# A two-layer graph kernel with residual and normalisation: its first row block done in four stripes, and column 0 loaded by chunk for four row blocks

## The reference

```
def _layernorm(x, axis=-1, eps=1e-05):
    m = jnp.mean(x, axis=axis, keepdims=True)
    v = jnp.var(x, axis=axis, keepdims=True)
    return (x - m) / jnp.sqrt(v + eps)

x_drop = x * (u >= 0.1) / 0.9                # x, u: (8192, 64)
h = _layernorm(x + adj @ x_drop)             # adj: (8192, 8192), float32
y = _layernorm(h + adj @ (h @ weight) + bias)   # weight: (64, 64)
```

## Time and profile before

| what | value |
|---|---|
| median of 3 runs | 946.46 us (946.38 to 946.99) |
| the profiled execution | 946.82 us |
| its span in the trace | 944.9 us |
| mean granted PE clock | 0.991 of full speed |
| PE busy | 911.6 us |
| DMA | 359.36 MB, 380 GB/s over the span |

### The profile page before, as it was taken

One profiled execution on the slowest core, in us unless ns is written; L12 is line 12 of the kernel. 1 busy time (PEld: TensorE's weight loads), 2 busy tenths in 40 slices (PEclk: granted clock), 3 DMA queues, 4 the chain that ended last, 5 costly groups with the idle time before them and its releaser, 6 DMA issues.

```text
span 944.9 us, 9819 instructions
## 1 busy us (share of the span) xinstructions
PE 911.6 (96%) x4288; PEld 307.0 (32%) x4288; DVE 202.8 (21%) x419; ACT 29.9 (3%) x68; POOL 24.1 (3%) x23
## 2 busy tenths in 40 slices
PE   4689999999999999999999999999999999999996
PEld 1123333333333333333333333333333333333342
DVE  2111121120131221312213120402122121130256
ACT  0010000000000000000000000000000000000011
POOL 2000000000000000000000000000000000000123
PEclk9799999999999999999999999999999999999998
DMA  9999999999969899799999999998989989999951
GB/s 349 402 421 421 419 421 421 421 385 423 420 273 422 335 377 421 307 421 387 349 412 389 421 363 421 368 421 327 422 343 397 420 347 421 420 418 421 395 225 67
DMA packets 57338, 359.36 MB, mean 380 GB/s; under 512 B 6352, under 2 KB 14544, under 8 KB 14544
## 3 DMA queue, kind: packets, MB, share of 16 engines
q1 hardware_dynamic: 57296, 358.74, 93.3%
HBM read 356.61 MB, written 2.10 MB: 380 GB/s over the span
## 4 chain that ended last, share of the span: by engine, by line
PE 92%; DMA 5%; SPq 3%; DVE 1%; issue 0%; ACT 0%; DVEq 0%
PE psum L586 26%; PE psum L631 22%; PE psum L591 21%; PE psum L615 18%; DMA tiles<-adj_t 5%; PE psum L637 3%; SPq L335 2%; PE psum L652 1%; PE psum L667 1%; SPq L314 1%; PE psum L596 0%; SPq L313 0%; DVE vsum L438 0%; DVE layer L544 0%; DVE rstd L444 0%
## 5 line engine op out<-in xcount | busy, mean ns | idle before, releaser
L591 PE MATMUL psum<-tiles,stat 128*64 128x512 f32 x548 | 252.7, 610 | 24.7 <-DMA tiles<-adj_t 24.7
L586 PE MATMUL psum<-tiles,stat 128*64 128x512 f32 x1136 | 253.3, 593 | 0.0
L596 PE MATMUL psum<-tiles,stat 128*64 128x512 f32 x548 | 252.7, 610 | 0.0
L631 PE MATMUL psum<-tiles,stat 128*64 128x512 f32 x944 | 210.7, 593 | 0.0
L474 DVE TENSOR_TENSOR layer<-psum,layer 128x512 f32<-128x512 f32 (+1 forms) x126 | 87.0, 690 | 461.1 <-PE psum L631 213.5
L615 PE MATMUL psum<-tiles,stat 128*64 128x512 f32 x768 | 169.1, 593 | 0.0
L591 PEld LDWEIGHTS psum<-tiles,stat 128*64 128x64 f32 x548 | 75.4, 140 | 191.0 <-issue 150.1
L586 PEld LDWEIGHTS psum<-tiles,stat 128*64 128x64 f32 x1136 | 80.7, 137 | 158.1 <-issue 158.1
L631 PEld LDWEIGHTS psum<-tiles,stat 128*64 128x64 f32 x944 | 67.2, 137 | 131.7 <-issue 130.9
L615 PEld LDWEIGHTS psum<-tiles,stat 128*64 128x64 f32 x768 | 54.8, 137 | 108.0 <-issue 108.0
L596 PEld LDWEIGHTS psum<-tiles,stat 128*64 128x64 f32 x548 | 75.4, 140 | 0.0
(11 more groups left out here) (38 smaller groups left out, 143.3 us busy)
## 6 DMA issues: line engine op xcount, KB each, us to landing
tiles<-adj_t SPq DMA_DIRECT2D x334, 1024.0 KB, 11.4
x_res<-x SPq DMA_DIRECT2D x16, 128.0 KB, 10.6
out<-layer SPq DMA_DIRECT2D x8, 256.0 KB, 2.1
tiles<-u SPq DMA_DIRECT2D x3, 512.0 KB, 14.0
tiles<-x SPq DMA_DIRECT2D x3, 512.0 KB, 15.2
tiles<-u SPq DMA_DIRECT2D x1, 384.0 KB, 6.2
tiles<-x SPq DMA_DIRECT2D x1, 384.0 KB, 7.3
tiles<-u SPq DMA_DIRECT2D x1, 128.0 KB, 2.0
```

What stands on the lines that cost most here:

```text
L586: last = pe.matmul(sum_a[i % 2][to, :], stat[:, j * C + c, half], tile[:, c], start=begun.get(("a", to.start)) != i, stop=False, skip_grou ...
L591: last = pe.matmul(sum_a[i % 2][low, :], stat[:, j * C + c, 0:D], tile[:, c], start=begun.get(("a", 0)) != i, stop=ends and c == 2, skip_g ...
L596: last = pe.matmul(sum_b[i % 2][high, :], stat[:, j * C + c, 0:D], tile[:, c], start=begun.get(("b", D)) != i, stop=ends and c == 3, skip_ ...
L631: last = pe.matmul(bank[to, :], stat[:, j * C + c, D:2 * D], tile[:, c], start=c == 0, stop=c == C - 1)
```

## The change

Row 0 is done in four stripes of 128 output rows. A stripe is four `part` jobs of four columns each, with matmuls that move 128 columns instead of 512 (64 of them in a stripe), and each stripe is copied out (`part_end`), transposed and normalised by itself (`part_turn`). That gives h of column 0 for chunk `c` = stripe alone. The tiles of row 0 come from a second array in HBM, `adj_0`: for columns 4 to 15 one load of 1 MiB holds one stripe of four tiles, and for columns 0 to 3, whose tiles are held whole for layer 2, each tile is loaded in four pieces of 256 KiB. Tiles of column 0 in rows 4 to 15 are no longer loaded whole: a load of 1 MiB takes chunk `c` of four of them, and its two jobs, `chunk` and `rest`, do both layers for two rows each (two halves each). Eight of the twelve such loads are placed into stripes 1 to 3; the `early` pairs of column 0 are gone. x and u are loaded all before the last load of stripe 0.

```diff
-XU_GROUPS = ((4, 5), (5, 8), (8, 12), (12, 16), (0, 4))
-XU_BEFORE = (1, 3, 6, 10)
+PARTS = 4
+XU_GROUPS = ((0, 1), (1, 4), (4, 8), (8, 12), (12, 16))
+XU_BEFORE = (1, 4, 5, 6)
...
+def chunk_jobs(c):
+    return [(kind, g, c) for g in range((NB - EARLY) // PARTS) for kind in ("chunk", "rest")]
...
+    for q in range(PARTS):
+        for g in range(groups):
+            jobs.append(("part", q, g))
+            if q and g == 0:
+                jobs.append(("part_turn", q - 1))
+            elif chunks_due and (q > 1 or g > 1):
+                jobs += chunks_due[:2]
+                chunks_due = chunks_due[2:]
+            if g == 0 and q:
+                chunks_due += chunk_jobs(q - 1)
+        jobs.append(("part_end", q))
+
+    for i in range(1, NB):
...
+        if i == 1:
+            heavy = chunks_due
...
+                if part is not None:
+                    to = tiles[:, slot, :, part * P:(part + 1) * P]
+                    source = adj_0[part, 0, :, tile[1]]
+                elif kind == "part":
+                    to, source = tiles[:, slot], adj_0[tile[1], tile[2]].rearrange("p k c b -> p k (c b)")
+                elif kind == "chunk":
+                    to = tiles[:, slot]
+                    rows = rows_of_chunk(tile[1])
+                    source = adj_t[rows.start:rows.stop, 0, :, tile[2]].rearrange("r p b -> p r b")
+                else:
+                    to, source = tiles[:, slot], adj_t[tile]
...
+                        for c in range(C):
+                            to, sums = (slice(0, D), sum_a) if c % 2 == 0 else (slice(D, P), sum_b)
+                            last = pe.matmul(sums[bank][to, 0:P], stat[:, j * C + c, 0:D], moving[:, c],
+                                             start=j == 0 and c < 2, stop=j == NB - 1 and c >= 2,
+                                             skip_group_check=True)
...
+                    for half in slice(0, D), slice(D, 2 * D):
+                        if n_second >= ECHO_BANKS:
+                            pe.wait_ge(added, n_second - ECHO_BANKS + 1)
+                        bank = echo[n_second % ECHO_BANKS]
+                        n_second += 1
+                        pe.matmul(bank[0:D, :], stat[:, c, half], moving[:, n], start=True, stop=True)
+                        last = pe.matmul(bank[D:P, :], stat[:, c, half], moving[:, n + 1], start=True, stop=True)
+                    last.then_inc(tile_jobs_done, 1)
...
+        "adj_0": np.ascontiguousarray(a[0].reshape(NB // PARTS, PARTS, P, C, PARTS, P).transpose(4, 0, 2, 1, 3, 5)),
```

More of the change, by code:

```diff
@@ L68, in seconds_of, with rows_of_chunk, first_row, turns @@
     return jobs
-TILE_JOBS = ("fused", "first", "second", "pair", "early")
-HALVES = {"first": 1, "second": 1, "fused": 2, "pair": 2, "early": 4}
+TILE_JOBS = ("part", "chunk", "rest", "fused", "first", "second", "pair", "early")
+HALVES = {"part": 1, "chunk": 1, "rest": 1, "first": 1, "second": 1, "fused": 2, "pair": 2, "early": 4}
 def tiles_of(job):
     kind, i, j = job
+    if kind == "part" and j == 0:
+        return [(0, k) for k in range(PARTS)]
+    if kind in ("part", "chunk", "rest"):
+        return [("chunk" if kind == "rest" else kind, i, j)]
     return [(i, j), (i + 1, j)] if kind in ("pair", "early") else [(i, j)]
+def rows_of_chunk(g):
+    return range(EARLY + PARTS * g, EARLY + PARTS * g + PARTS)
+def first_row(job):
+    return rows_of_chunk(job[1])[0 if job[0] == "chunk" else 2]
+def chunk_jobs(c):
+    return [(kind, g, c) for g in range((NB - EARLY) // PARTS) for kind in ("chunk", "rest")]
+def turns(i):
+    return i + PARTS
 def begins_at(i):
@@ L97, in put @@
         nonlocal lead
-        if job[0] in ("first", "fused", "early"):
+        if job[0] == "rest":
+            n = 0
+        elif job[0] in ("first", "fused", "early", "chunk"):
             n = len(tiles_of(job))
@@ L110, in order_of_work @@
         heavy = [("fused", i, j) for j in range(begins_at(i), i - 1) if i >= 2]
[L111 to L124, removed]
+        if i == 1:
+            heavy = chunks_due
+        filler = []
+        while sum(HALVES[job[0]] for job in filler) < FILL:
+            choice = [heavy, early] if lead < LEAD else []
+            choice = [jobs_of for jobs_of in (*choice, light, again, heavy, early, near) if jobs_of]
+            filler.append(choice[0].pop(0))
+            put(filler[-1])
+            if len(filler) == 1:
+                jobs.append(("turn", i - 1) if i > 1 else ("part_turn", PARTS - 1))
+        if i == 1:
+            heavy += chunk_jobs(PARTS - 1)
+        for job in seconds_of([r for r in range(NB) if held(r, i - 1)], i - 1):
+            put(job)
+        again += seconds_of([r for r in range(i - 1) if not held(r, i - 1)], i - 1)
+        if 1 <= i - 1 < EARLY:
+            early = sorted(early + [("early", r, i - 1) for r in range(EARLY, NB, 2)], key=lambda job: job[1:])
         if has_fused(i):
@@ L317, in _ @@
             rows_begun = 0
-            for n, (i, j, slot, use, freed, kind) in enumerate(loads):
+            for n, (tile, part, slot, freed, new, kind) in enumerate(loads):
                 if n in XU_BEFORE:
@@ L511, in _ @@
                 elif job[0] == "turn":
[L512 to L529, removed]
+                    turn(turns(job[1]) - 1, job[1], slice(0, C))
                 elif job[0] == "final":
@@ L556, in arrived, with h_of @@
             def arrived(job, tile):
[L558 to L559 removed]
+                slot, load = place[job, tile]
+                pe.wait_ge(s_arrived[slot], 16 * load)
                 return tiles[:, slot]
+            def h_of(turned_rows):
+                nonlocal h_seen
+                if turned_rows > h_seen:
+                    pe.wait_ge(h_ready, turned_rows)
+                    h_seen = turned_rows
             for at, job in enumerate(jobs):
```

188 lines of the change are left out of this document (133 added, 55 removed).

## The result

| | before | changed |
|---|---|---|
| median | 946.6 us (4 runs) | 986.13 us (985.48 to 986.7, 4 runs) |
| profiled execution, span | 946.82, 944.9 us | 985.48, 983.7 us |
| PE busy | 911.6 us | 926.2 us |
| last wait of PE for a load in the opening stage | 72.66 us | 184.23 us |
| span behind that wait | 872.2 us | 799.5 us |

The changed kernel takes 1.0414 times as long (1.0401 to 1.0427): 4.1% slower. The prediction said 947.3 us, 941.5 to 955. It missed by 39 us.

A forecast was written before the change was run, and what follows sets the result against it. Loads bound the opening stage, PE the rest, so the last load wait decides. Pieces cost 6.0 us, early work gains 5.2: +0.8 us, span 945.7, execution 947.6, less 0.4 profiled over median: 947.3 us, range 941.5 to 955.

The forecast's parts named there:

- What bounds it, and where it is decided: Opening stage: loads set the time until PE's last load wait, moving from 72.66 us to job `first` (2, 9).
- The change, the pieces of the loads: Loads ahead of (2, 9): 4 MiB in 512-byte and 12 MiB in 2 KiB runs cost 6.0 us extra.
- The upper bound: Of the pieces' cost: a 512-byte packet as dear as a 1 KiB one, 15.7 us.
- The sizes themselves: Packet time of 7.7 ns + 0.0368 ns a byte: 512 bytes 3.39, 2 KiB 2.66 us a MiB, against 2.47.
- The line's test by 256-byte packets: A window read as nearly all 256-byte packets gave 16.8 ns a packet, where the packet-size formula gives 17.1.
- The early work's gain: Before (2, 9), more halves done during load-bound time: 72.1 + 0.7 - 67.6 = 5.2 us gained.
- PE: Stripe jobs at 0.13 us a 128-column pair; PE is there at 143.4 us, 2.8 before the loads, so hidden.
- rival C: PE decides: pairs slower than 0.143 us or longer half clock; 950.6 us at 0.16, 968.7 at 0.247; chance 0.30.
- The half clock: In stripe 0 after PE's waits: two `part` jobs at half pace add 4.2 us to PE's sum, hidden behind loads.
- B: Short runs are cheap, engines go by bytes or by the 2 KiB read: 944.4 us, down to 941.3; chance 0.26.
- D: Loads starve PE later, the lead at 140 us being gone; 0.8 to 2.5 us a tile, 949 to 952; chance 0.06.
- PE's tenths: Profile page of the kernel before: read as 9 everywhere except in the first three slices.

The follow-up runs named there:

- e12: Changed kernel word for word, but the host pads each row of tiles so rows lie 17 MiB apart instead of 16: 949.2 us, 1.0026 of before.
- e7: Changed kernel with chunk loads from a padded array: rows still 16 MiB apart, partitions 2 KiB apart instead of 8: 950.29 us, 1.0036 of before.
- e6: Changed kernel with chunk loads from a copy of column 0: partitions still 8 KiB apart, rows 1 MiB instead of 16: 949.39 us, 1.0027 of before.
- e2: Changed kernel with chunk loads from an own array, each 8 KiB a partition in one run: 947.52 us, 1.0006 of before.
- e4: Kernel with dense chunk loads, plus row 0's 16 pieces written as one 2 KiB run a partition instead of 512-byte runs: 944.19 us, 0.997 of before.
- e10: Kernel with dense chunks, 2 KiB pieces and 57 spare transposes, plus x and u stored by partition: 941.6 us, 0.9945 of before.
- experiment 1: DMAs alone, no kernel work, nine phases of 12 MiB in different patterns: 2 KiB runs 387 to 389 GB/s in four patterns, 512-byte runs 290.
- e11: Kernel before the change with only x and u stored by partition: 945.63 us, 0.9986 of before.
- e8: Kernel with dense chunks and 2 KiB pieces, plus 57 spare transposes in stripe 0's waits against half clock: 944.31 us against 944.19 without them.

## Why the prediction was wrong

Each kernel's last wait and its span give one table. If only that wait decides, the difference is constant.

| kernel | last wait | span | difference |
|---|---|---|---|
| changed | 184.23 | 983.7 | 799.5 |
| `e12` rows 17 MiB apart | 148.28 | 947.7 | 799.4 |
| `e7` | 148.74 | 948.2 | 799.5 |
| `e6` | 147.86 | 947.3 | 799.4 |
| `e2` chunk loads dense | 146.12 | 945.6 | 799.5 |
| `e4` pieces dense too | 143.14 | 942.6 | 799.5 |
| `e10` x and u too | 140.63 | 940.1 | 799.5 |

- **What bounds it, and where it is decided: right.** The job of the last wait, `first` (2, 9), and what lies behind it hold in all seven.
- **The change, the pieces of the loads: this step failed**, in the price of the 12 chunk loads. It took a packet's time from its size alone, 83.1 ns for 2 KiB, from rows in which no load skips through HBM in steps of many MiB. In place it was 5.7 us a MiB, not 2.66: 12 x 3.0 = 36 us of the 38.0 by which the last wait came late; the 2 us that remain are there without the chunk loads' layout too (next points). The upper bound failed in the same way: it made only the 512-byte packets dearer.
- **The sizes themselves: right, one of their tests by luck.** 12 MiB in 2 KiB runs cost 1.7 to 2.6 us in `e6`, `e7` and `e12` (2.3 worked out). 4 MiB in 512-byte runs against 2 KiB ones cost 2.98 us in `e4`, where the working gives 4 x (3.39 - 2.66) = 2.9. The rule of the Trainium skill (DMA: Bandwidth & Descriptors, key figures) that line rate begins at 512 bytes does not hold here: 290 GB/s against 425 for whole tiles in experiment 1. The line's test by 256-byte packets was misread. In that window 0.31 MB went in 390 packets, so most bytes can't have gone in packets of 256 bytes; by the packet records 27 of 8 KiB and more filled about 70% of the engines' time. That 16.8 ns came out near the line's 17.1 was luck. The 256-byte packets themselves took 18 ns, so the line stands all the same (in the 1 KiB window 908 packets, not 932, were of that size, which changes nothing), and so do the medians of the changed kernel, 27 ns for 512 bytes and 84 ns for 2 KiB.
- **The early work's gain: right in kind, 2.1 us too large.** The working without any cost of pieces puts the last load at 140.25 us. `e4` has 143.14, and about 0.8 us of it are the pieces' 2 KiB runs (4 x 0.19): 2.1 us late, the same 2 us as in the changed kernel. The gain over before is then 944.9 - 942.6 + 0.8 = 3.1 us on the spans, for 5.2 worked out. The windows show where this arises; before and `e4` first, then both with packed x and u (`e11`, `e10`):

```profile
0.00:40.00 40.00, 23.64 (x76) 6.38 (x78) 8.45 (x8) 1.28 (x1) 6.89 (x8) 0.91 0.97 368
0.00:40.00 40.00, 20.14 (x227) 17.46 (x229) 13.36 (x22) 3.29 (x5) 6.89 (x8) 0.83 0.96 346
...
0.00:40.00 40.00, 23.35 (x80) 6.16 (x80) 6.35 (x8) 1.28 (x1) 6.90 (x8) 0.91 0.95 379
0.00:40.00 40.00, 26.84 (x294) 21.96 (x294) 13.83 (x23) 3.30 (x5) 6.89 (x8) 1.00 0.95 369
```

  In the first 40 us, while x and u are loaded, `e4` moves 22 GB/s less than before, which is 2.1 us of loading at 420 GB/s; from 40 to 110 us the two are at 417 and 420. With packed x and u the gap is 10 GB/s. So about half of it goes with x and u, which the change loads earlier and in other company. The rest was not taken apart.
- **PE: rival C did not come.** 16 pairs of 128 columns take 1.97 us, (1.97 - 0.27) / 15 = 0.113 us a pair, under the 0.13 taken, though a weight load takes 0.14 us. The weight loads of the job at 35.12 us run beside its matmuls, 32 of them in 1.73 us:

```profile
35.12 1.73 PEld L691 LDWEIGHTS psum<-tiles,stat 128*64 128x64 f32 x32 [0.46 <-DMA tiles<-adj]
```

  So the rule of the Trainium skill (TensorE: Matmul & The Clock Gate, Part 3), by which these loads would not hide, does not hold for 128 columns either. The half clock was there as forecast and cost nothing (`e8`). In the changed kernel PE fell to half clock again after some of the long waits (3.50 us at 43, 3.95 at 63), not after all (3.31 at 136); `e12` has full clock in its window at 58 us, where the loads are quick.
- **Rivals B and D:** B (runs as cheap as whole tiles) did not come, `e2` against `e4` shows what 512-byte runs cost. D (starved later) neither, since the difference in the table is constant.
- **A small misreading:** PE's tenths are 9 outside the first three slices but for the last, which is 6 before and after; it lies behind the last wait and changes nothing.

What stays open is what in HBM makes the clash. Shown is that it depends on the addresses: on the distance between rows (slow at 4, 8, 16 and 32 MiB, at full rate at 1, 15 and 17), and on which of the loads are in flight together. That it also needs the 8 KiB between partitions is likely from `e7` and from phases 1 and 4 of experiment 1 (338 and 388 GB/s), but there the neighbours in the queue moved as well. Whether another order of the chunk loads alone would have cured the kernel, as it does for loads alone (191 to 354), was not run. How addresses are spread over HBM, no trace shows.

## What to carry to other kernels

Price a strided load by its addresses as well as by its run length: rows of before with the same packet size but other distances do not bound it. If a load gathers from places a large power of two apart (here 4 to 32 MiB), lay the pieces side by side in HBM, or put a gap (here one tile in 17) between the rows; and put the distance into the range of a forecast as long as no row shows it. When a window of packets is to test a price, check by its bytes that the packets are what fills its time. Where a stage is bound by loads, find the last wait for one and add what lies behind it: that sum gave each variant's span to 0.1 us.

## What the runs showed of the hardware

- Loads of 1 MiB in runs of 2 KiB, partitions 8 KiB apart, rows 16 MiB apart: 191 GB/s in the kernel's order, with neighbours in the queue 64 MiB apart. With rows 1, 15 or 17 MiB apart 387 to 389. With neighbours in the queue 2 MiB apart, rows 4, 8, 16 and 32 MiB apart run at 316 to 333, 2 MiB at 370. (For 1 MiB they were 4 MiB apart.)
- The slowness sits in a minority of packets: the median 2 KiB packet takes 84 ns at 191 GB/s and at 354, but 28% against 5% take over 150 ns.
- A queue of such loads looks busy: a share of 0.91 in the phase that moves 191 GB/s.
- Runs of 512 bytes 290 GB/s, 2 KiB 387, 8 KiB 425.
- Weight loads of 0.14 us hide behind matmuls of 128 columns on the same rows, a pair each 0.113 us.
